# The first attention's sine rows issued by GpSimd instead of by SP and ScalarE

## The reference

```python
xh = x.reshape(B, S, H, dh)                       # H = 16 heads of dh = 16
theta_q = xh / (1.0 + jnp.abs(w_q)) + b_q + t * phi_q
sin_q, cos_q = lookup_sin_cos(theta_q)
Q = jnp.concatenate([cos_q, sin_q], axis=-1)      # K in the same way, with w_k, b_k, phi_k
V = cos_v + sin_v
scores = jnp.einsum('bqhd,bkhd->bhqk', Q, K) / scale
attn = softmax(where(causal, -inf, scores))
out = einsum('bhqk,bkhd->bqhd', attn, V)          # then cos + sin of an angle of out, added to x
```

## Time and profile before

| | |
|---|---|
| runs | 1037.24, 1037.89, 1038.05 us; median 1037.89 |
| profiled execution | 1038.47 us, span 1036.7 us |
| TensorE (PE) busy | 901.0 us, 87% of the span |
| VectorE (DVE) busy | 733.1 us, 71% |
| ScalarE (ACT) busy | 578.8 us, 56% |
| GpSimd (POOL) busy | 238.3 us, 23% |
| mean granted TensorE clock | 0.954 |
| first attention | about 0 to 269 us of the span |

### The profile page before, as it was taken

One profiled execution on the slowest core, in us unless ns is written; L12 is line 12 of the kernel. 1 busy time (PEld: TensorE's weight loads), 2 busy tenths in 40 slices (PEclk: granted clock), 3 DMA queues, 4 the chain that ended last, 5 costly groups with the idle time before them and its releaser, 6 DMA issues. The chain is left out here.

```text
span 1036.7 us, 21581 instructions
## 1 busy us (share of the span) xinstructions
PE 901.0 (87%) x8634; PEld 556.8 (54%) x8634; DVE 733.1 (71%) x1416; ACT 578.8 (56%) x1036; POOL 238.3 (23%) x234
## 2 busy tenths in 40 slices
PE   1477989898488799999689999997899988999997
PEld 0232434243247555565356777776799974455554
DVE  7899888533779899887668899885778855344412
ACT  4579898887375555453145555553788853332410
POOL 1000000000256030000256667675244110000000
PEclk9989989899689899999799999998899999999999
DMA  5404141410410030000310000000200000000001
GB/s 146 82 1 65 19 64 21 58 26 2 162 43 2 1 133 1 1 2 1 116 51 3 2 2 2 2 2 1 72 3 2 3 1 1 1 17 6 21 1 41
DMA packets 21602, 30.43 MB, mean 29 GB/s; under 512 B 5936, under 2 KB 17918, under 8 KB 20352
## 3 DMA queue, kind: packets, MB, share of 16 engines
q1 hardware_dynamic: 18752, 26.44, 11.0%
q10 hardware_dynamic: 2752, 2.62, 0.9%
HBM read 18.56 MB, written 2.10 MB: 20 GB/s over the span
## 5 line engine op out<-in xcount | busy, mean ns | idle before, releaser
L580 ACT ACTIVATE t_pT<-t_sc 128x1536 f32<-128x1536 f32 x96 | 136.5, 1454 | 31.6 <-PE t_sc L694 18.2
L688 PE MATMUL t_sc<-t_qk 32*128 32x512 f16 (+3 forms) x1152 | 85.8, 350 | 42.7 <-DMA t_qk<-t_sin_parts 22.2
L3205 PE MATMUL f_psh<-f_h,fs_w 128*128 128x512 f16 x512 | 114.4, 379 | 1.5 <-DVE f_h L3149 1.5
L3149 DVE SCALAR_TENSOR_TENSOR f_h<-f_psh,f_h 128x512 f16<-128x512 f32 x64 | 43.9, 691 | 100.8 <-ACT f_h L3175 100.7
L3175 ACT ACTIVATE f_h<-f_psh 128x512 f16<-128x512 f32 x64 | 38.2, 597 | 108.4 <-PE f_psh L3205 108.4
L688 PEld LDWEIGHTS t_sc<-t_qk 32*128 32x128 f16 x1152 | 35.7, 97 | 99.1 <-issue 46.0
L2668 POOL TENSOR_SCALAR_AFFINE_SELECT r_att<-r_att 128x1024 f16<-128x1024 f16 x64 | 69.5, 1108 | 68.8 <-DVE r_att L2708 68.7
L711 PE MATMUL t_ot<-t_pT,t_v 128*17 128x512 f32 (+3 forms) x768 | 78.3, 520 | 5.2 <-issue 4.0
L3205 PEld LDWEIGHTS f_psh<-f_h,fs_w 128*128 128x128 f16 x512 | 49.8, 98 | 59.0 <-issue 2.0
L1964 PE MATMUL c_pso<-ck_VO,c_pT 128*128 128x256 f16 x480 | 55.0, 273 | 1.4 <-DVE c_pT L1815 1.4
L2708 DVE TENSOR_TENSOR r_att<-r_pss,r_att 128x1024 f16<-128x1024 f32 x32 | 39.1, 1221 | 20.6 <-ACT r_att L2834 20.6
(11 more groups left out here) (526 smaller groups left out, 2126.5 us busy)
## 6 DMA issues: line engine op xcount, KB each, us to landing
t_qk<-t_cos_parts SPq DMA_DIRECT2D x24, 128.0 KB, 5.4
t_qk<-t_sin_parts SPq DMA_DIRECT2D x24, 128.0 KB, 7.0
x<-in_x ACTq DMA_DIRECT2D x4, 512.0 KB, 7.4
out_x<-x SPq DMA_DIRECT2D x4, 512.0 KB, 2.9
r_rcos<-in_ret_cos SPq DMA_DIRECT2D x1, 1280.0 KB, 9.2
r_rsin<-in_ret_sin SPq DMA_DIRECT2D x1, 1280.0 KB, 10.9
t_qk<-t_cos_parts SPq DMA_DIRECT2D x16, 64.0 KB, 2.8
gw_raw<-in_gateT SPq DMA_DIRECT2D x1, 1024.0 KB, 7.6
```

Of the source, the lines that this page charges most:

```text
L580: a.activation(pT[:, at:at + 3, :].rearrange("p a s -> p (a s)"), sc[s % 2][:], ACT.Exp, scale=CURVE * CURVE / math.sqrt(2 * DH)).then_inc ...
L688: last = t.matmul(sc[s % 2][:, 512 * k + at:512 * k + at + w], qk[r, g % 3, 1, of_k, P * i:P * i + P], qk[r, g % 3, 0, of_q, q0:q0 + w], s ...
L3149: v.scalar_tensor_tensor(dst[:, 1], psh[:, i % BANKS, :], 0.0, dst[:, 0], ALU.max, ALU.subtract).then_inc(lo_done, 1)
L3205: last = mm(psh[:, i % BANKS, :], l, r, start=(k == 0), stop=(k == len(todo) - 1))
```

## The change

SP issues the cosine rows of all quads, GpSimd the sine rows of all quads, ScalarE none. The sine transfers count on semaphores of their own, `first_swept` and `swept`, so each wait for `first` or `moved` gets a second one beside it, and each semaphore counts to half of what it did. GpSimd issues those of group 0 ahead of `inverse_root(1)` and the others behind it. In the first half GpSimd issues quad 0 and quad 1, and then the same for the second half.

```diff
         def moves_of(g):
-            return 16 * 8 * (g // 3 + 1 + (g % 3 == 1))
+            return 16 * 4 * (g // 3 + 1 + (g % 3 == 1))
@@ sync
-            def move(g, c, lo, hi, done):
-                for dst, src in moves(g, c, lo, hi):
-                    sp.dma_start(dst, src).then_inc(done, 16)
-
             for h in range(2):
+                sp.wait_ge(bent, 2 * pieces_of(0, h) - 1)
                 for g in range(2):
-                    for c in range(2):
-                        if g == 0 and c == 1:
-                            continue
-                        sp.wait_ge(bent, 2 * pieces_of(0, h) - 1 + c)
-                        move(g, c, 512 * h, 512 * h + 512, moved[g] if h or g else first)
+                    for dst, src in moves(g, 0, 512 * h, 512 * h + 512):
+                        sp.dma_start(dst, src).then_inc(moved[g] if h or g else first, 16)
             for n in range(1, GROUPS):
                 for g in (2 * n, 2 * n + 1):
                     if g >= 3:
                         sp.wait_ge(filled, LAST_EXP(g - 3))
-                    for c in range(2):
-                        if g == 2 * n:
-                            sp.wait_ge(bent, 2 * pieces_of(n) - 1 + c)
-                        move(g, c, 0, S, moved[g % 3])
+                    sp.wait_ge(bent, 2 * pieces_of(n) - 1)
+                    for dst, src in moves(g, 0, 0, S):
+                        sp.dma_start(dst, src).then_inc(moved[g % 3], 16)
@@ gpsimd
+            for h in range(2):
+                g.wait_ge(bent, 2 * pieces_of(0, h))
+                for quad in range(2):
+                    for dst, src in moves(quad, 1, 512 * h, 512 * h + 512):
+                        g.dma_start(dst, src).then_inc(swept[quad] if h or quad else first_swept, 16)
             inverse_root(1)
+            for n in range(1, GROUPS):
+                for quad in (2 * n, 2 * n + 1):
+                    if quad >= 3:
+                        g.wait_ge(filled, LAST_EXP(quad - 3))
+                    g.wait_ge(bent, 2 * pieces_of(n))
+                    for dst, src in moves(quad, 1, 0, S):
+                        g.dma_start(dst, src).then_inc(swept[quad % 3], 16)
@@ vector, parts_free
                     v.wait_ge(moved[g % 3], moves_of(g))
+                    v.wait_ge(swept[g % 3], moves_of(g))
                 if n == 1:
-                    v.wait_ge(first, 16 * 8)
+                    v.wait_ge(first, 16 * 4)
+                    v.wait_ge(first_swept, 16 * 4)
@@ scalar
-            def move_sines(h):
-                a.wait_ge(bent, 2 * pieces_of(0, h))
-                for dst, src in moves(0, 1, 512 * h, 512 * h + 512):
-                    a.dma_start(dst, src).then_inc(moved[0] if h else first, 16)
...
-                move_sines(h)
@@ tensor, exp_step
-                    t.wait_ge(first, 16 * 8)
+                    t.wait_ge(first, 16 * 4)
+                    t.wait_ge(first_swept, 16 * 4)
...
                     t.wait_ge(moved[g % 3], moves_of(g))
+                    t.wait_ge(swept[g % 3], moves_of(g))
```

More of the change, by code:

```diff
@@ L162, in table_attention @@
         first, moved = sem("first"), [sem(f"moved{k}") for k in range(3)]
+        first_swept, swept = sem("first_swept"), [sem(f"swept{k}") for k in range(3)]
         v_pre, v_waves, v_ready = (sem(n) for n in ("v_pre", "v_waves", "v_ready"))
```

## The result

| | before | after |
|---|---|---|
| runs shown ahead of the prediction | 1037.89 us (3) | |
| median of all runs beside each other | 1036.72 us (20 runs, 1034.04 to 1041.64) | 1040.43 us (20 runs, 1038.25 to 1048.56) |
| profiled execution, span | 1038.47, 1036.7 us | 1041.44, 1039.7 us |

The ratio is 1.0037, interval 1.0022 to 1.0052: the change costs 3.7 us. The forecast was 1038.2 and no change; the time lies in the stated range, and the case that came true is on the slower side, which had 0.38.

A forecast was written before the change was run, and what follows sets the result against it. TensorE was taken to bound the attention, its late start at step 2 shifting all that follows. +0.1 (step 2), +0.1 (quad 2) and +0.1 (waits) gave +0.3 us, a median of 1038.2 us, no change; range 1035.2 to 1045.

The forecast's parts named there:

- the slower side: Whole kernel slower by over 2.1 us: Rival 1, some of Rival 3 and quad 2's ceiling together; chance 0.38.
- ScalarE's 4.9 us: Opening: without its eight sine issues ScalarE finishes exp 0 4.9 us earlier, worth only what the sines' landing lets through.
- step 2: Opening, TensorE's exp step 2, waiting for quad 0's second-half sines: start 44.86 against 44.78 us, +0.1, from -2.3 to +7.0.
- Rival 1: Opening: a GpSimd issue costs 1.3 us or more, twelve in a row; +4.1 at 1.45 us, +7.0 at the ceiling; chance 0.30.
- c: Time of one sine transfer issue on GpSimd, taken as 1.1 us, between 0.6 and 1.66.
- my floor of 0.6: Lower bound in us for one GpSimd issue, from the same transfer on ScalarE's queue at 0.62 to 0.83.
- Quad 2 and quad 6: Later groups, TensorE's waits for sines: quad 2 +0.1 us, from -1.55 to +1.9; quad 6 hidden by 0.5 us of cover.
- my ceiling of 1.9: Upper bound in us for quad 2's added wait, if the queues' turns give cosines two for one.
- signs of being wrong: In the profile after: issues beyond 1.3 us, gaps beside VectorE's fast instructions, long landing, quad 2 or 6 waiting more.
- The +0.1 us for the second waits: TensorE and VectorE get a second semaphore wait beside each first: nothing or 0.1 us overall, clearing four more semaphores included.
- Rival 2: GpSimd issues at 0.75 us: -1.5 at step 2, another -1.0 at quad 2, giving 1035.4 us; chance 0.16.
- Rival 3: Opening: GpSimd's issues stand still beside VectorE's fast instructions; +1.1 to +2.5 us, 1039.0 to 1040.4; chance 0.16.

The follow-up runs named there:

- e3: The whole change, but SP holds the cosines of quads 3, 5 and 7 until the preceding quad's sines landed; 1038.43 us against 1036.83 before, ratio 1.0021.
- e5: The whole change plus 18 dummy TensorE matmuls ahead of the waits for quads 2 and 6; 1038.82 us against 1037.64 before, ratio 1.0012.
- e11: The whole change plus dummy TensorE matmuls, 30 ahead of quad 2's wait and 54 ahead of quad 6's; 1039.85 us against 1036.77 before, ratio 1.003.
- e1: The change in group 0 (quads 0 and 1) alone, sines of groups 1 to 3 on SP as before; 1035.63 us against 1036.83 before, ratio 0.999.
- e9: Group 0's sines by GpSimd, later groups all SP's, high parts of quads 2, 4, 6 sent early; 1032.38 us against 1036.77 before, ratio 0.996.
- e4: The whole change with queues swapped in groups 1 to 3: GpSimd issues cosines, SP sines; 1050.25 us against 1036.83 before, ratio 1.0131.
- e6: The change, but in groups 1 to 3 SP carries heads 0 and 1, GpSimd heads 2 and 3; 1041.21 us against 1037.64 before, ratio 1.0046.
- e7: As e6, with group 0 also split by heads and quad 1 moved behind both halves of quad 0; 1044.4 us, ratio 1.0064 to the kernel before.

## Why the prediction was right and wrong

**Right.** The time lies in the range, on a mechanism that was only in part the one forecast. Right was that ScalarE's eight issues held back the second half and VectorE with it: the second half's Sin ran at 29.50 without a wait for issues, exp 0 at 37.96 (forecast 38.3), and VectorE lost its idle time there. That none of ScalarE's 4.9 us is worth more than the sines' landing lets through: step 2 waits for sine rows and nothing else. That inverse_root(1) isn't delayed. Rival 1, the slow issue, was excluded: c is 0.50 us on the page, for the 24 issues of the later groups, and 0.58 and 0.62 on the mean of the two eights of group 0 (4.61 and 4.92 us), held ones included; an issue that nothing holds is below my floor of 0.6.

**Step 2: +0.1 forecast, -1.1 measured.** The term was mis-sized in two parts that partly cancel, and a third was missing. I took the middle between an issue on another queue and a power on GpSimd, 1.1 us; it is 0.51, and the eight first issues are over at 33.8, long before the second half. The landing went the other way: 2.2 us from the end of an issue forecast, 3.3 measured (issue at 39.7 to 40.2, landed at 43.5), with both queues at work on 64 KB transfers. My 2.6 from the earlier trace rows was itself read too long: that issue took 0.83 us and not 0.6, which leaves 2.3. What wasn't in the sum: GpSimd's issues begin 0.3 us behind the rows they wait for, at 38.20 behind VectorE's end at 37.90,

```profile
36.68 1.22 DVE L379 TENSOR_TENSOR t_sin_parts<-t_sines,t_sin_parts 128x1024 f16<-128x1024 f32 x1
```

where ScalarE's had begun 0.03 us behind theirs. For the issue the nearer row was that of the same operation, not that of the same engine.

**Quad 2 and quad 6: +0.1 and nothing forecast, and this is the step that failed.** The prediction said that if the two queues take turns the last sine is the eighth transfer behind the first cosine instead of the seventh. That was wrong by its own words: four sines that take turns with four cosines have three or four of these ahead of the last one, not one. And by my own c of 1.1 us the fourth sine would have been issued from 96.1, 0.9 us later than before, not over a microsecond sooner; it went out at 93.5. The queues do share, and more than one got ahead: when quad 2's last sine landed at 101.9, two of quad 3's cosines were in and others of both queues under way. The rate went up, which I had left at 127 to 139 GB/s: 169 and 170 in the rows above. The two together leave 0.7 to 1.2 us of lateness (e3 shows whose), within my ceiling of 1.9. Its price was sized wrongly because I took the wait as its whole cost: with the clock, quad 2 lost 2.2 us in the profile, beyond that ceiling. At quad 6 0.5 us of cover was too thin for it, and at both quads the clock fell behind the standstill, 1.6 and 1.1 us in the profile. e5 and e11 tie these two falls to the standstills. The prediction had no term for the clock at all. A longer wait at quad 2 or 6 stood among its signs of being wrong, and it came. The +0.1 us for the second waits was not tested by any run.

**Luck.** The forecast was +0.3 us, and +3.7 was measured. The time looks nearer, 2.2 us above the forecast, because the kernel before was 1.2 us faster over 20 runs than over the three that the forecast stood on. And the gain that was missed at the opening hides part of the loss that was missed at the quads. How much of the 3.7 us is waiting and how much the clock stays open, since only single profiles separate them.

**Rival 2 (quick issue) had the right cause and the wrong end.** It named 1035.4 for an issue of 0.75 us, -1.5 at step 2 and -1.0 at quad 2. The first came nearly so, the second came with the other sign. e1 is that rival with only its first half, and gives its gain: 0.999.

**Rival 3 (VectorE holds GpSimd up) is real and off the path.** GpSimd's fifth issue of the second half, and VectorE's instruction beside it, both in the profile after:

```profile
40.20 0.93 POOL L267 DMA_DIRECT2D t_qk<-t_sin_parts  x1
...
40.33 0.69 DVE L327 TENSOR_SCALAR t_tmp<-t_va 128x1024 f32<-128x1024 f32 x1
```

The issue takes 0.93 us instead of 0.51 and ends at 41.13, 0.11 us after VectorE's instruction; the eighth, at 42.13, takes 0.99 and ends 0.11 us after another of that kind, from 42.32 to 43.01. So VectorE's fast pace does hold an issue, until it is done, at 0.4 to 0.5 us each time. In group 0 it hit the first issue (1.01 us from 29.17) and these two; the four that step 2 waits for, 38.20 to 40.20, lay between. The Trainium skill, "SBUF — State Buffer", section "SBUF: two separate sides", says that a GpSimd descriptor write waits until the VectorE instruction's end and about 115 ns more; the trace agrees with both. The price here, 0.51 us grown to 0.93 to 1.01, is well under the step from 620 to 3100 ns that the Trainium skill gives in that section for a transfer beside a VectorE copy.

## What to carry to other kernels

A second queue for transfers doesn't only save issue time: here it let work that isn't urgent overtake onto the DMA engines. Before moving half of a stream to another queue, look for what the first queue will issue in the freed time and whether it is needed before the half that moved. What helped most here was not a queue but sending what was ready earlier (e9). Where a wait ahead of TensorE has less cover than a microsecond, count a lower clock behind it in the price, and don't count on a gain ahead of a wait until you know that the rows behind it come sooner too.

## What the runs showed of the hardware

- GpSimd mostly issued a 16-partition transfer in 0.48 to 0.51 us, faster than SP and ScalarE (0.6), when VectorE leaves it alone.
- Over the same stretches two queues moved more between SBUF rows than one: from 92 to 98 us 169 GB/s with the change, against 143 before and 150 in e1; from 96 to 102 us 178 against 128. The Trainium skill, "DMA: Bandwidth & Descriptors", section "Issuing engines are not separate DMA queues", says that issuing on several engines saves only the sequencer's time; for these 16-partition transfers the measured rate rose by an eighth to two fifths.
- The two queues weren't served alike: 0.76 MB for GpSimd's and 0.30 for SP's in 6 us of the change, 0.75 and 0.20 in e4. Beside GpSimd's transfers many of SP's issues stretched from 0.6 us to between 1 and 2.5 (e4, e6, e7); issues of 1.63 and 1.11 us stand in the kernel before too. Why wasn't tried; whether it would be the same with ScalarE's queue is open too.
- The granted clock went from 2.4 to 1.2 GHz behind standstills of 1.8 and 2.2 us and stayed up where dummy matmuls filled them or cut them to 1.24 us and less (e5 at quad 2, e11). Other falls came at other places; how they are chosen stays open. Single runs of the kernel before differ by 7.6 us; whether these falls are the reason isn't shown.
